# Macaron block on one core: a new order for the last five tiles, two search states, and weight loads in SyncE's queue

## What is computed

```python
def _L0_ffn_ref(x, A, B, Wr):          # K, TOPK, RANK = 64, 16, 16
    scores = xf @ Wr.T
    top_vals, top_idx = jax.lax.top_k(scores, TOPK)
    gates = jax.nn.softmax(top_vals, axis=-1)
    ...
    h = jnp.einsum('nd,krd->nkr', xf, A)
    out = jnp.einsum('nkr,kdr->nd', h * G[:, :, None], B)

def _L0_attn_ref(x, w_gate, w_up, w_down):     # I = 1376, k = 688
    s = jax.nn.silu(jnp.einsum('bsh,ih->bsi', x, w_gate))
    _, idx = jax.lax.top_k(-jnp.abs(s), k)     # the k smallest of a row become 0
    ...
    s = s * jnp.einsum('bsh,ih->bsi', x, w_up)
    return jnp.einsum('bsi,hi->bsh', s, w_down)

x = x + 0.5 * _L0_ffn_ref(_layernorm(x), ...)
x = x + _L0_attn_ref(_layernorm(x), ...)
x = x + 0.5 * _L0_ffn_ref(_layernorm(x), ...)
```

## Time and profile before

| | us |
|---|---|
| median of 3 runs (lowest to highest) | 745.86 (743.34 to 747.37) |
| profiled execution | 749.87 |
| its span in the trace | 747.8 |
| PE busy | 705.0 (94%) |
| DVE busy | 476.1 (64%) |
| ACT busy | 360.9 (48%) |
| POOL busy | 215.4 (29%) |

### The profile page before, as it was taken

How to read it: one execution, slowest core, us unless ns; L and a number is a source line. 1 busy time by engine, 2 the same in 40 slices (tenths; PEclk the granted TensorE clock), 3 DMA queues, 4 the chain that set the end, 5 groups by cost and what they waited for, 6 DMA issues and landing times.

```text
span 747.8 us, 10322 instructions
## 1 busy us (share of the span) xinstructions
PE 705.0 (94%) x3683; PEld 334.5 (45%) x3683; DVE 476.1 (64%) x1003; ACT 360.9 (48%) x458; POOL 215.4 (29%) x544
## 2 busy tenths in 40 slices
PE   5996999999999999999999999999999999979685
PEld 2443444445444444545444444544444444434231
DVE  5996787658585666567476566657475656554631
ACT  6756785555545352544635353554535264554200
POOL 4121325332315042323415042322404132422000
PEclk9998999999999999999999999999999999999898
DMA  8785523151634171524324241523423241413321
GB/s 318 226 170 118 135 57 72 25 109 41 126 68 94 36 108 29 110 57 88 79 50 94 52 95 43 96 56 71 82 45 66 56 82 29 82 28 68 67 57 42
DMA packets 170522, 62.27 MB, mean 83 GB/s; under 512 B 163632, under 2 KB 163632, under 8 KB 170464
## 3 DMA queue, kind: packets, MB, share of 16 engines
q1 hardware_dynamic: 167952, 51.01, 33.6%
q0 software_dynamic: 2512, 10.55, 4.4%
HBM read 16.97 MB, written 4.19 MB: 28 GB/s over the span
## 4 chain that ended last, share of the span: by engine, by line
PE 72%; DVE 8%; ACT 5%; DMA 5%; POOL 5%; issue 4%; SPq 0%; DVEq 0%; POOLq 0%; ACTq 0%
PE ps L533 14%; PE ps L534 14%; PE ps L535 14%; PE ps L625 10%; PE ps L626 10%; PE ps L629 10%; ACT signs L806 3%; DMA pt_hi<-p_hi 2%; POOL small L447 2%; DVE mem L1129 1%; DVE small L1131 1%; DMA mem<-mem 1%; DMA mem<-w_a 1%; POOL small L445 1%; POOL small L443 1%
## 5 line engine op out<-in xcount | busy, mean ns | idle before, releaser
L806 ACT ACTIVATE signs<-mem,small 128x1376 bf16<-128x1376 f32 x112 | 161.4, 1441 | 154.8 <-POOL small L447 131.9
L625 PE MATMUL ps<-w_b_hi,pt_hi 128*128 128x512 f16 x256 | 98.5, 385 | 6.8 <-DMA pt_hi<-p_hi 5.8
L533 PE MATMUL ps<-w_a_hi,xt_f 128*128 128x512 f16 x256 | 98.9, 386 | 1.7 <-DVE w_a_lo L1013 1.7
L534 PE MATMUL ps<-w_a_hi,xt_f 128*128 128x512 f16 x256 | 98.8, 386 | 0.0
L535 PE MATMUL ps<-w_a_lo,xt_f 128*128 128x512 f16 x256 | 98.8, 386 | 0.0
L626 PE MATMUL ps<-w_b_lo,pt_hi 128*128 128x512 f16 x256 | 98.5, 385 | 0.0
L533 PE MATMUL ps<-w_u_hi,xt 128*128 128x512 f16 (+1 forms) x192 | 69.2, 360 | 2.5 <-DVE mem L1108 2.5
L535 PE MATMUL ps<-w_u_lo,xt 128*128 128x512 f16 (+1 forms) x192 | 69.0, 359 | 0.0
L534 PE MATMUL ps<-w_u_hi,xt 128*128 128x512 f16 (+1 forms) x192 | 69.0, 359 | 0.0
L534 PE MATMUL ps<-w_g_hi,xt 128*128 128x512 f16 (+1 forms) x192 | 68.5, 357 | 0.0
L535 PE MATMUL ps<-w_g_lo,xt 128*128 128x512 f16 (+1 forms) x192 | 68.5, 357 | 0.0
(11 more groups left out here) (140 smaller groups left out, 1235.1 us busy)
## 6 DMA issues: line engine op xcount, KB each, us to landing
x<-x SPq DMA_DIRECT2D x14, 256.0 KB, 2.9
out<-x SPq DMA_DIRECT2D x14, 256.0 KB, 2.3
mem<-w_g POOLq DMA_DIRECT2D x4, 688.0 KB, 9.2
mem<-w_u POOLq DMA_DIRECT2D x4, 688.0 KB, 5.5
mem<-w_d POOLq DMA_DIRECT2D x5, 512.0 KB, 4.6
mem<-w_a SPq DMA_DIRECT2D x4, 512.0 KB, 6.1
mem<-w_b POOLq DMA_DIRECT2D x4, 512.0 KB, 7.3
pt_hi<-p_hi SPq DMA_TRANSPOSE x32, 3.2
```

Source lines behind the costliest of these rows:

```text
L533: pe.matmul(dst, x_hi, w_hi, start=start, stop=False)
L534: pe.matmul(dst, x_lo, w_hi, start=False, stop=False)
L625: pe.matmul(dst, x_hi[:, c, :], hi[m.name][:, c, :], start=c == 0, stop=False)
L806: act.activation(signs[:, :], mags[t % 2], ACT.Sign, bias=thr, scale=-1.0, accum_out=bal).then_inc(counted, 1)
```

## The change

It has five parts.

1. The last five tiles, called `a, b, c, e, f` (11 to 15), get a new order on all five engines. On PE `gates(14)` comes before `down(12)` and `gates(15)` right behind `ups(14)`; the flags of tiles 14 and 15 are summed in the middle of an `experts` block (`flags_of`), and the last `combine`s stand one block later than their `experts`.
2. The search state exists twice, by the parity of the tile: `mag_sum`, `thr`, `bal`, `off`, `far`, `move`, `steps`, and the semaphores `thr_ready` and `counted`. `aim(t)` now waits for the flag of tile t - 2.
3. `gated(14)` is cut in two: `gated_begun` frees the first two of the three banks once `ups(14)` has filled them (`up_begun`), so `gates(15)` can start; its last third waits for `gated_ended`.
4. The last but one `combine` writes a bank of the gates (`comb_bank`), which is free by then, so the last one needs to wait only for the addition two before it.
5. All weight loads are issued by SyncE, between its other DMAs: `w_b` behind x1, `w_g` behind x3, the pieces of `w_u` and `w_d` between turns (`load_u`, `load_d`), each with the wait for the part of the staging area that it overwrites.

```diff
+        tops = sb("tops", [P, 32], F32)
+        top_a, top_b, cand8, evens = (tops[:, 8 * n:8 * (n + 1)] for n in range(4))
...
+        mag_sum, thr, bal, off, far, move = (
+            [col(n + str(h)) for h in range(2)]
+            for n in ("mag_sum", "thr", "bal", "off", "far", "move"))
...
+        def comb_bank(k):
+
+            return bank(WIDE if k == len(calls) - 2 else COMB)
...
+            def load_u(n):
+
+                last = (n + 1) * I - 1
+                if last < AT_B:
+                    wait_low(sp, MA, len(MA.pieces) - 1)
+                else:
+                    wait_low(sp, MB, MB.piece_of((last - AT_B) // D))
+                load_w(MU, n)
+
+            def load_d(n):
+
+                c, k, rows = MD.pieces[n]
+                wait_low(sp, MG, min(((c + k) * D - 1) // I, DC - 1))
+                load_w(MD, n)
...
-            load_w(MR)
-            load_w(MA)
+            load_w(MR, 0)
+            load_w(MA, 0, 1, 2, 3)
             load_x(1)
+            load_w(MB, 0, 1, 2, 3)
             load_x(2)
             load_x(3)
+            load_w(MG, 0, 1, 2, 3)
+            load_x(4)
             turn_x(1, 2)
-            load_x(4)
+            load_u(0)
             turn_p_hi(0)
             turn_x(1, 3)
+            load_u(1)
             turn_p_lo(0)
+            load_u(2)
+            turn_p_hi(1)
             load_x(5)
             load_x(6)
-            turn_p(1)
+            turn_p_lo(1)
+            load_u(3)
             turn_p_hi(2)
             turn_x(1, 4)
             turn_p_lo(2)
             turn_x(2, 0)
-            turn_p(3)
+            turn_p_hi(3)
+            load_d(0)
+            load_d(1)
+            turn_p_lo(3)
+            load_d(2)
...
             def aim(t):
 
+                h = t % 2
                 pool.wait_ge(mag_ready, t + 1)
-                if t:
-                    pool.wait_ge(flag_ready, t)
...
+                if t >= 2:
+                    pool.wait_ge(flag_ready, t - 1)
...
+                if k == len(calls) - 2:
+                    pe.wait_ge(val_ready, NT)
+                elif k == len(calls) - 1:
+                    pe.wait_ge(added, k - 1)
+                elif k:
                     pe.wait_ge(added, k)
...
+                last = t == NT - 1
+                if last:
+                    pe.wait_ge(val_begun, 1)
...
+            a, b, c, e, f = range(FULL, NT)
+            down(a)
+            gates(c)
+            combine(3, a - 1)
+            sum_flags(b)
+            ups(c)
+            experts(3, a)
+            gates(e)
+            down(b)
+            ups(e, flags_of=c)
+            gates(f)
+            combine(3, a)
+            down(c)
+            experts(3, b, flags_of=e)
+            ups(f)
+            down(e)
+            experts(3, c, flags_of=f)
+            combine(3, b)
+            down(f)
+            experts(3, e)
+            combine(3, c)
+            experts(3, f)
+            combine(3, e)
+            combine(3, f)
...
+            counts(e, 3, 4)
+            tanh(f)
+            count(e, 5)
+            magnitude(f)
+
+            act.wait_ge(counted[e % 2], rounds_before(e) + ROUNDS - 1)
+            count(f, 0)
+            act.wait_ge(counted[f % 2], rounds_before(f) + 1)
+            count(e, 6)
+            act.wait_ge(counted[e % 2], rounds_before(e) + ROUNDS)
+            counts(f, 1, 2, 3)
+            v_to_hi(e)
...
+            def gated_begun(t):
+
+                dve.wait_ge(gate_ready, t + 1)
+                dve.wait_ge(up_begun, 1)
+                dve.scalar_tensor_tensor(out=val[:, 0:2 * BANK], in0=gate[:, 0:2 * BANK], scalar=VAL_S,
+                                         in1=bank(WIDE, 2 * BANK), op0=ALU.mult, op1=ALU.mult
+                                         ).then_inc(val_begun, 1)
```

More of the change, by code:

```diff
@@ L614, in experts @@
                     for o in range(2):
+                        if o and flags_of is not None:
+                            sum_flags(flags_of)
                         for c in range(DC):
@@ L650, in wide @@
                         norms(norms_of)
+                    if behind is not None and o + BANK >= I:
+                        pe.wait_ge(val_ready, behind)
                     w = min(BANK, I - o)
@@ L1439, in _ @@
[L1439 to L1443 removed]
+            a, b, c, e, f = range(FULL, NT)
+            add_ffn(1, f)
+            norm_stats(2, e)
+            select(b)
+            mask(b)
+            norm_apply(2, e)
+            x_to_lo(2, e)
+            add_down(a)
+            norm_stats(3, a)
+            silu(c)
+            norm_apply(3, a)
@@ new lines, in _ @@
+            x_to_lo(3, a)
+            add_ffn(3, a - 1)
+            check(b)
+            norm_stats(2, f)
+            v_to_lo(b)
+            norm_apply(2, f)
+            gated(c)
+            x_to_lo(2, f)
+            choose(number[3, a])
+            route(number[3, a])
+            apply_route(number[3, a])
+            p_to_lo(number[3, a])
+            silu(e)
+            select(c)
+            mask(c)
+            add_down(b)
+            norm_stats(3, b)
+            gated_begun(e)
@@ new lines, in _ @@
+            check(c)
+            gated_ended(e)
+            norm_apply(3, b)
+            v_to_lo(c)
+            x_to_lo(3, b)
+            silu(f)
+            select(e)
+            add_down(c)
+            mask(e)
+            norm_stats(3, c)
+            check(e)
+            norm_apply(3, c)
+            add_ffn(3, a)
+            v_to_lo(e)
+            choose(number[3, b])
+            x_to_lo(3, c)
+            route(number[3, b])
+            apply_route(number[3, b])
+            gated(f)
```

344 lines of the change are left out of this document (154 added, 190 removed).

## The result

| us | before | after |
|---|---|---|
| median (lowest to highest) | 746.62 (743.34 to 749.98, 4 runs) | 714.99 (714.26 to 716.07, 4 runs) |
| profiled execution | 749.87 | 715.56 |
| its span | 747.8 | 713.7 |

The changed kernel takes 0.9577 of the time of before (95% interval 0.9543 to 0.9611), 31.6 us less. The forecast was 711.1 us, with a range from 705 to 720.

The account below looks back on a forecast made before the run. PE was taken as full from 125 to 578 us, leaving only the ends: head 6.2 + tail 28.6 = 34.8 us off the profiled 749.87 gives 715.1, less 4.0 makes a median of 711.1 us, range 705 to 720.

Parts of the forecast that it names:

- Head, 6.2 us: Start up to the gate matmuls: `p_to_hi(3)` and the last square 4.6 us earlier, 1.6 us from the clock.
- The share above one at few GB/s: DMA engines early on: share above one at 140 GB/s with transposes among loads, read as the mixture being slow.
- Rival (b): Weight loads at the head: moving them brings nothing, transposes stay slow near any load; 717.3 us, chance 0.09.
- The middle, nothing: Between 125 and 578 us: PE busy 451.19 of 453 us, only fewer columns could shorten it; no gain.
- Tail, 28.6 us: From `down(11)` on: 137.5 us against 166.15, with waits gone and the clock at 1.00.
- Tile 13 has from 14.1 to `sum_flags` in the middle of `ups(14)` at 51: wide.: Tail: tile 13's search fits between these times T, in us after `down(11)` starts, so no wait for its flag.
- The tight one: Tail, tile 15's search: flag at T = 92 us after `down(11)` starts, between 90.4 and 95.2, wanted at 94.7.
- rival (c): Search in the tail: doubling its state does nothing, tail worth half, 14.3 us; 725.4 us, chance 0.04.
- From the profiled run to the median, 4.0 us: Whole kernel: profiled run before lies 4.0 us above the median of three runs, so 715.1 becomes 711.1.
- (a): Last tiles: the search still sets the pace, late flags stop PE and lower the clock; 719 us, chance 0.12.
- (d): From 26 to 80 us: turns queue behind weight pieces, 8.2 us more each; slower at 752 us, chance 0.03.
- What was to show it: Signs: norms of `w_u` wait under 2.5 us, turn under 4, tail waits under 3, clock 1.00, tail 136 to 139.

Follow-up runs that it names:

- experiments 4 and 5: Kernel before with `w_u` loads issued early, still in GpSimd's queue: 745.52 us; changed kernel with them issued late, in SyncE's queue: 714.56 us.
- experiment 3: Changed kernel with one search state instead of two, `aim(t)` waiting for the flag of tile t - 1, PE's order kept: 726.94 us, ratio 0.9711.

## Why the prediction was right, and where not

- **Head, 6.2 us: right in the trace, less at the medians.** 6.4 measured between the two traces. `p_to_hi(3)` was put near 54.8 and started at 54.71, the gap at 1.8 and was 1.39, the turn at 3.3 and took 3.0, the clock came back. That the slow landing came from loads in GpSimd's queue beside the turns was shown by experiments 4 and 5, with the reserve told there. At the medians the loads' move brought 3.2 us on the old tail and 4.5 on the new. Early turns land up to 2.6 us later behind a piece (5.6 against 3.0), more than the 1.9 us that I had as the most, but no wait of PE shows it, so the cost of nothing stood. The share above one at few GB/s, which I read as the mark of the mixture, is no such mark: from 38 to 40 us the changed kernel has 1.26 at 201 GB/s, with one queue. Rival (b) is out: it would have put the changed kernel's head at 70 us.
- **The middle, nothing: missed by 2.1 us.** The range's low end allowed for it ("some waits after 125 us gone"), but no step derived it. The doubled state worked on tiles 1 and 2 too. I had costed it only in the tail, and took the 1.8 us that the earlier trace rows miss between 125 and 578 us for nothing that the change touches.
- **Tail, 28.6 us: 3.0 too much.** The failing step is "Tile 13 has from 14.1 to `sum_flags` in the middle of `ups(14)` at 51: wide." In the trace the flag of tile 13 is written at 620.59, T = 50.8, only 1.0 us before PE is through the first part of `ups(14)`; what stood behind its last count and its select on two in-order engines came late. The step asked only whether the flag is ready in time. `sum_flags` also writes the bank of `down` and so waits for the last `add_down`, a wait that I had put at nothing: 1.40 us at tile 13's flag and 0.67 at tile 14's, with 0.43 at `ups(14)` and 0.17 at `gates(15)` 2.7 in all. The tight one I named, tile 15, held: its flag was written at 666.30, T = 96.5, or 93.9 without the waits before it (I had taken 92, between 90.4 and 95.2), and PE came to it 1.6 us later. PE's work was right: with two calls swapped the tail took 137.2 us, where the sum says 137.5. The cost of 0 to 1 us at `gates(15)` was 0.17.
- **The doubling: worth more than I thought.** Without it the changed kernel takes 12.0 us more, 10.0 of them in the tail and 2.0 in the middle (experiment 3); rival (c), that it does nothing, is out. (That its 725.4 us is near the 726.9 of experiment 3 is chance: the rival has the whole change come out there, and the whole change took 715.0.)
- **From the profiled run to the median, 4.0 us: this is what missed.** The forecast of the profiled execution was 715.1 and it took 715.56: the 3 us of the tail and the 2.1 and 0.2 elsewhere nearly cancelled, so that sum was good partly by luck. I then took off 4.0 us, the distance of the profiled run from the median of before. After the change that distance is 0.6, and the forecast came out 3.9 us low, 3.4 of them by this step. The 4.0 were no constant of the machine. About half of them came from a median of only three runs: over all 38 runs of the kernel before in four sessions the median is 747.8 us, 2.1 below the profiled run. The rest belongs to a kernel whose runs lie 6 to 10 us apart, where the changed one's lie within 1.8. What makes the old kernel's runs differ stays open, since both of its traces (749.87 and 749.78 us) are longer than nearly all of those runs.
- **Rivals (a) and (d): out.** No flag of tile 14 or 15 is waited for, and the slowest turn from 26 to 60 us takes 5.6 us with none on PE's path.
- **What was to show it:** turn and norms as said; PE's waits in the tail 3.2 us where under 3 was said; the tail 140.5 us where 136 to 139 was said; the clock of the last stretch 0.99 where 1.00 was said.

## What to carry to other kernels

Where a transposing DMA of SyncE lands late, look for plain loads that run beside it from GpSimd's queue, and put both into one queue before touching their times. When margins of a search or chain are checked for a new order, check also the short instructions that stand behind it on in-order engines: here one tanh behind one count cost 1.8 us, and fitted into a wait of its own engine. A distance between the profiled run and the median belongs to the kernel as it is, and a median of three runs that spread over 4 us is itself off by microseconds; carry it into a forecast only if its cause is known and stays.

## What the chip showed that I had not expected

**GpSimd's small steps stretch beside VectorE.** The last instruction of a search step (L493, 128x1) takes 0.34 us as a rule, and 1.34 us at 607.38, beside `p_to_lo`; 1.68 at 620.70, beside the mask; 2.33 at 628.19, beside `v_to_lo`. Of its 96 executions in the changed kernel 17 took over 0.6 us; 11 of them began beside a `p_to_lo` pass, five beside another VectorE pass whose large inputs lie in SBUF, or within 0.12 us ahead of it, and one beside small VectorE steps only. No short one began beside `p_to_lo`, but 14 short ones beside the `gated` pass, which reads PSUM. In the kernel before it is 13 of 15 beside `p_to_lo`. This is how the traces coincide; no run took a pass away to show it. The Trainium skill ("GPSIMD Engine Reference", section "Specifications") has GpSimd share its SBUF interfaces with VectorE, "contention with DVE instructions in a 2-port perf mode or with two SBUF inputs"; by that rule the `p_to_lo` pass (two SBUF inputs) should hold a step up and the `gated` pass (one in PSUM) should not, and the trace agrees with both.

**During the slow turns the DMA engines are not idle.** The Trainium skill ("SBUF — State Buffer", section "SBUF: two separate sides") knows loads from GpSimd's queue that stall because VectorE locks GpSimd out, with the DMA engines idle meanwhile. That is not what is seen here: the DMA share was 1.53 at 140 GB/s while the turn of 11.5 us was under way. By this share packets were on their way all the time and moved little.
